# Four fused transformer sub-layers on one core: the last delta chunk taken one sequence at a time and without its state, the output weights split inside the attention, and first tokens normalised by halves of the sequences

## The reference

```python
x = x + delta_attention(layernorm(x))   # 6 heads of 64, causal conv, gated delta rule, Wo
x = x + nvfp4_ffn(layernorm(x))         # 4-bit weights, gelu(gate) * up, hidden 4096
x = x + latent_attention(layernorm(x))  # 16 heads, latent 64, rotary, softmax over 1024, wo
x = x + sparse_ffn(layernorm(x))        # silu(gate) * up, two largest of each four kept, hidden 2048
```

```python
S = S * exp(g_t)
u = b_t * (v_t - k_t @ S)
S = S + outer(k_t, u)
o_t = (q_t * scale) @ S
o = o * rsqrt(mean(o*o) + EPS) * o_norm_w * silu(gate)      # then @ Wo.T
```

## Time and profile before

| | |
|---|---|
| median of 3 runs | 3021.94 us (3019.69 to 3023.62) |
| profiled execution | 3021.52 us, span 3019.7 us |
| mean granted clock of TensorE | 0.961 of full speed |
| PE busy | 2829.2 us, 94% of the span |
| DVE, ACT, POOL busy | 56%, 36%, 26% |
| DMA | 114.92 MB, mean 38 GB/s |

### The profile page before, as it was taken

The page is one execution under the profiler, slowest core; times in us unless marked ns, Lnnn a source line. Parts: engine busy times, 40 slices in busy tenths (PEclk is TensorE's granted clock), DMA queues, the critical chain, the costliest instruction groups (busy, mean ns, idle before and its releaser), DMA issues. The chain is left out here.

```text
span 3019.7 us, 37185 instructions
## 1 busy us (share of the span) xinstructions
PE 2829.2 (94%) x13750; PEld 2332.9 (77%) x13750; DVE 1702.2 (56%) x2585; ACT 1073.9 (36%) x1615; POOL 791.4 (26%) x832
## 2 busy tenths in 40 slices
PE   7966988799999999999999689999999899999998
PEld 7846777678888888888888558888888677888887
DVE  6864677564445444454543666666666256545554
ACT  3343343131121211111211357777777522212221
POOL 0038686100000000000000157777778510000000
PEclk9967999899999999999999889999999999999999
DMA  2243232110000100000100121111110100101001
GB/s 85 104 115 70 52 73 49 46 42 21 22 21 21 42 21 21 21 21 21 35 7 1 40 64 43 43 43 36 43 36 22 43 14 28 42 1 42 14 14 42
DMA packets 96418, 114.92 MB, mean 38 GB/s; under 512 B 47072, under 2 KB 73696, under 8 KB 94624
## 3 DMA queue, kind: packets, MB, share of 16 engines
q1 hardware_dynamic: 96288, 113.20, 12.7%
HBM read 86.16 MB, written 26.74 MB: 37 GB/s over the span
## 5 line engine op out<-in xcount | busy, mean ns | idle before, releaser
L2017 POOL TENSOR_TENSOR att_p_lo<-att_probs,att_p_hi 128x768 fp32r<-128x768 f32 x256 | 467.3, 1837 | 147.3 <-ACT att_p_hi L2074 146.1
L2170 DVE TENSOR_REDUCE att_top<-att_q_scores 128x1 f32<-128x1024 f32 x250 | 305.5, 1222 | 220.0 <-PE att_q_scores L2277 187.9
L271 DVE TENSOR_TENSOR fp_hidden<-fp_gelu,fp_up 128x512 f32<-128x512 f32 x128 | 88.0, 687 | 440.2 <-PE fp_up L75 377.2
L2085 ACT ACTIVATE att_probs<-att_k_scores 128x1024 f32<-128x1024 f32 x256 | 262.9, 1027 | 160.9 <-PE att_k_scores L2295 159.5
L1751 POOL MEMSET lat_power<- 128x16 f32 x1 | 0.1, 111 | 1051.8 <-POOLq L52 1051.8
L256 DVE TENSOR_TENSOR k_stream<-k_stream,fp_down 128x512 f32<-128x512 f32 x256 | 175.4, 686 | 89.6 <-PE fp_down L75 86.1
L335 ACT ACTIVATE fp_gelu<-fp_gate 128x512 f32<-128x512 f32 x128 | 76.4, 597 | 420.3 <-PE fp_gate L75 419.4
L2074 ACT CAST att_p_hi<-att_probs 128x768 fp32r<-128x768 f32 x256 | 211.7, 827 | 0.0
L73 PE MATMUL fp_gate<-fp_feat_hi,fp_w_hi 128*128 128x512 f32 x512 | 200.6, 392 | 4.0 <-DVE fp_feat_lo L241 4.0
L2277 PE MATMUL att_q_scores<-att_k_stack,att_q_stack 128*128 128x512 f32 x500 | 187.1, 456 | 14.5 <-DMA att_q_stack<-att_k_stack 10.6
L75 PE MATMUL fp_gate<-fp_feat_hi,fp_w_lo 128*128 128x512 f32 x512 | 200.2, 391 | 0.0
(11 more groups left out here) (350 smaller groups left out, 6537.3 us busy)
## 6 DMA issues: line engine op xcount, KB each, us to landing
f_early<-codes SPq DMA_DIRECT2D x16, 768.0 KB
f_early<-scales SPq DMA_DIRECT2D x16, 768.0 KB
la_values<-w_sparse SPq DMA_DIRECT2D x10, 1024.0 KB, 5.2
f_early<-qkv SPq DMA_DIRECT2D x16, 576.0 KB, 6.2
att_q_stack<-rotated SPq DMA_DIRECT2D x128, 64.0 KB, 2.6
att_k_stack<-rotated SPq DMA_DIRECT2D x128, 64.0 KB, 2.6
qkv<-f_early SPq DMA_DIRECT2D x12, 512.0 KB, 2.9
k_stream<-hidden SPq DMA_DIRECT2D x4, 1024.0 KB, 10.3
```

The lines of the kernel that those rows point to most:

```text
L2017: pool.tensor_tensor(p_lo[:, buffer, :], probs[:, slot, 0:SPLIT], p_hi[:, buffer, :].bitcast(F32), ALU.subtract).then_inc(lo_done, 1)
L2085: act.activation(probs[:, t, :], k_scores[:], ACT.Exp).then_inc(exp_done, 1)
L2170: dve.tensor_reduce(top[buffer][:, STACK + t:STACK + t + 1], scores[:], AX.XY, ALU.max, negate=True).then_inc(max_done, 1)
```

## The change

It has four parts.

1. Last delta chunk: `decay_state`, `add_to_state` and `add_state` are left out for chunk 7 (no later chunk reads the state). Its sums, gate, logarithms and normalisation are done for sequence 0 and then for sequence 1. The second `first_codes` stands after `corrected_values` as before. The turned outputs go to other PSUM banks (3 and 4), so that PE waits for one sequence's `gated` only. SP issues the codes and scales before the residual of chunk 6.
2. First tokens of both feed-forwards: the token blocks are taken in the order 0, 2, 1, 3, and `EARLY` is now the first half of both sequences (tiles 0 to 3 and 8 to 11). The first four tiles of the 4-bit stage are scaled before that stage (`scale_first`), into the storage of the delta rule's blocks; the Gelu table is loaded there too.
3. `w_out` is loaded into the rotary tables' storage during the attention's pass 6, and split in its last pass: for each of the four heads a 128x512 cast on ACT at t = 3 and a 128x512 subtraction on DVE at t = 4. Silu's table is loaded at the start of `project_out`.
4. Sparse stage: in the first group `scale` of block tb + 2 stands after the four products of block tb. Several buffers share storage with buffers of the attention.

```diff
@@ delta_rule, sync @@
+                if c == LAST:
+                    sp.wait_ge(qk_ps, FOURS * CHUNKS)
+                    load_codes(sp, fp4, codes, scales, 0)
                 if c:
                     load_residual(c - 1)
...
-            sp.wait_ge(qk_ps, FOURS * CHUNKS)
-            load_codes(sp, fp4, codes, scales, 0)
             load_residual(CHUNKS - 1)
@@ delta_rule, tensor @@
-                    else:
-                        pe.wait_ge(gated, 2 * c + 2)
-                        pe.wait_ge(state_done, 6 * CHUNKS)
...
-                add_to_state(c, ahead)
+                if c != LAST:
+                    add_to_state(c, ahead)
@@ delta_rule, scalar @@
-            output_logs(CHUNKS - 1)
-            split_output(CHUNKS - 1)
+            act.wait_ge(o_small, 4 * LAST)
+            for b in range(BATCH):
+                last_square(b)
+                last_logs(b)
+            split_output(LAST)
+            act.preload_act_table(ACT.Gelu_apprx_tanh)
@@ delta_rule, vector @@
+            def scale_first():
+                dve.wait_ge(token_norm.rstd_done, 1)
...
+                for j, i in enumerate(tiles_of(0)):
+                    dve.tensor_scalar(fp4.normed[:, j, :], stream[:, i, :], token_norm.mean[:, i:i + 1],
+                                      token_norm.rstd[:, i:i + 1], ALU.subtract, ALU.mult).then_inc(fp4.normed_done, 1)
...
                 corrected_values(c)
-                if c == CHUNKS - 1:
-                    first_codes(1, (0, 1))
-                gate_output(c)
-                decay_state(c)
-                add_state(c)
-            output_sums(CHUNKS - 1)
-            normalise_output(CHUNKS - 1)
+                if c != LAST:
+                    gate_output(c)
+                    decay_state(c)
+                    add_state(c)
+            first_codes(1, (0, 1))
+            last_sums(0)
+            last_gate(0)
+            last_normalise(0)
+            last_sums(1)
+            last_gate(1)
+            last_normalise(1)
             first_codes(1, (2,))
-            low_output(CHUNKS - 1)
-            token_stats(CHUNKS - 2)
+            low_output(LAST)
+            token_stats(LAST - 1)
+            scale_first()
@@ nvfp4_feed_forward, scalar @@
-            act.preload_act_table(ACT.Gelu_apprx_tanh)
@@ softmax_heads, sync, scalar, vector @@
+                if g == QUAD * (PASSES - 2) + 1:
+                    sp.wait_ge(piece_step, 3 * ROTATED)
+                    sp.dma_start(o32.rearrange("p (k n) -> p k n", k=KT), w_out.rearrange("(k p) n -> p k n", p=P))\
+                      .then_inc(o_in, 16)
...
+                        if t == 3 and last:
+                            high_weights(j)
...
+                        if t == 4 and last:
+                            low_weights(j)
                         if t == TURN and not (last and j == QUAD - 1):
                             copy_top(g + 1, False)
@@ project_out, scalar, vector, tensor @@
-            act.wait_ge(o_in, 16)
-            act.copy(o_hi[:], o32[:]).then_inc(o_hi_done, 1)
+            act.preload_act_table(ACT.Silu)
...
-            pe.wait_ge(o_lo_done, 1)
@@ sparse_feed_forward, vector @@
-                    for i in next_tiles:
-                        scale(i)
...
+                    if first and tb + 2 < BLOCKS:
+                        if tb == 0:
+                            dve.wait_ge(norm.rstd_done, 2)
+                        scale(tb + 2)
```

More of the change, by code:

```diff
@@ L348, in _ @@
             high_weights(0, 0, 1)
[L349 to L350 removed]
+            high(0)
             body(0, True, False)
@@ L2697, in body @@
                     act.wait_ge(kept, 4 * n + 4)
-                    act.copy(h_hi[:], hidden[:]).then_inc(h_hi_done, 1)
-            for i in range(SUB):
-                high(i)
+                    act.copy(h_hi, hidden).then_inc(h_hi_done, 1)
+            high(0)
             body(0, True, False)
```

284 lines of the change are left out of this document (167 added, 117 removed).

## The result

| | before | changed |
|---|---|---|
| median | 3021.94 us (11 executions, 3014.32 to 3028.03) | 3009.42 us (11 executions, 3001.32 to 3012.33) |
| profiled execution, span | 3021.52 us, 3019.7 us | 3001.32 us, 2999.5 us |
| mean granted clock | 0.961 | 0.964 |
| PE busy | 2829.2 us, 94% | 2825.2 us, 94% |

The changed kernel is faster: ratio 0.9958, 95% interval 0.9949 to 0.9968, which is 12.5 us of the 21.95 that I had forecast. 3009.4 lies outside the range of 2995 to 3007.

The account below looks back on a forecast made before the run. PE, busy 94% of the span, was taken as the bound. From 3021.52 us, less 6.5, 3.4, 1.3, 8.45 and 4.6, plus 2.3, gives 2999.6; with the median 0.4 above, 3000.0 us, range 2995 to 3007 (8 in 10).

Parts of the forecast that it names:

- what is paid for it lies in the last pass: Last attention pass: casts and subtractions of `w_out` quarters cost 2.3 us, bounds 0.5 and 4.4.
- if the last pass grows by over 4 us: Last attention pass: growth above this size was one of three signs that the prediction is wrong.
- codes: Last delta chunk: earlier issue lets scales land sooner, PE idles less and outputs keep their clock; 6.5 us saved.
- chain: Behind the last delta outputs: first projection matmul follows after 6.75 us, not 10.13; 3.4 us saved.
- table load: Head of the stage after the delta rule: load moves from ahead of the weight cast to ACT's idle time; 1.3 us saved.
- The boundary of `project_out`: Start of `project_out`: PE no longer waits for load, cast and subtraction of `w_out`; 8.45 us saved.
- The sparse scaling: Sparse stage: tiles scaled earlier, so PE goes on at about 2502.1, not 2506.73; 4.6 us saved, bounds 3.5 and 5.4.
- A new wait at a boundary: Rival, 12%: a stage's head is bounded by something the old wait covered; up to 6 us together, near 3005.
- The transfer was not late: Rival, 12%: delta chunk 7's scales still land at 570 or later; 6.5 us gone, 3006.5.
- Half clock over `project_out`: Rival "Slower", 2%: `project_out` begins in small pieces and TensorE stays at half clock; some 43 us, result 3043.

Follow-up runs that it names:

- storage_swap: Changed kernel with the sparse stage's third high weight part and `h_hi` exchanging places in SBUF; 3007.8 us, one execution.
- no_part3: Changed kernel with `w_out` loaded, cast and subtracted at the start of `project_out`, ahead of PE's transposes; median 3008.5 us, ratio 0.9964.
- sub_behind_copy: Changed kernel with the last pass's quarter subtraction of the output weights behind `copy_top` instead of ahead of it; median 3001.6 us, ratio 0.9939.
- half_ahead: Changed kernel with each last-pass quarter subtraction cut into 256-column halves, one ahead of `copy_top`, one behind; median 3011.3 us, ratio 0.9964.
- split_incs_first: Changed kernel with `w_out` split whole at `project_out`'s start, DVE's opening increments ahead of its wait for the cast; median 3004.0 us, ratio 0.9944.

## Why the prediction came out wrong

**The step that failed** is the one headed "what is paid for it lies in the last pass": "A 128x512 quarter [...] is 0.5 on ACT and 0.6 on DVE", so 2.3 us back, with 4.4 as the upper bound. ACT's part measured 0.62. DVE's 0.6 was scaled from an operation that ran while POOL was idle (2.29 us for four quarters); in the pass POOL is at work, and the quarter takes 1.9. In place of 2.3 the runs show 7.4 us (the mean of C over the nine profiles with a whole quarter ahead of the copy, 94.8, against 87.4). Of that 3.2 us are two waits of PE for `copy_top` (I had priced a delay in three heads), 1.7 are time lost at half clock behind the first wait, in all nine profiles, and 3.4 more are lost behind the second wait in four of the nine; I had not priced the clock there. Some 0.9 us are shorter waits of PE in the last two heads. The bound was too narrow because both its ends used the same row. I had named this in the text as the thing that would prove me wrong ("if the last pass grows by over 4 us").

**Not in the sum at all**: column F, 1.8 us, the down products of the sparse stage; and G, 1.1 us, where the last down products run at half clock for 5 to 6 us in most profiles instead of 3.5, after the same wait of 4.3. Part of the change is the new place of buffers, which I had costed at nothing without saying so. What slows the down products is not settled. That G is due to the change is only likely: both before are at 20.6, twelve of the fourteen others at 21.5 or more, but storage_swap and no_part3 at 20.7.

**Right in mechanism and size**: codes, chain and table load, 11.2 us together: B falls from 110.4 (two profiles) to 98.3 (nine), 12.2. Within it the outputs fell by 2.9 us by the clock between the first two profiles (3.1 forecast), the chain to 6.4 us (6.75), the table 1.14 (1.3). Less sure is the codes' own share: with only their order undone the tail grows by 3.6 and 5.0 us, and I had put 6.5. The boundary of `project_out`: 8.45 forecast, 8.7 measured. The sparse scaling: 4.6 forecast; E, which also holds `project_out`, fell by 3.8, undoing the part costs 3.0 to 3.8, and the blocks themselves show 5.5 less the 1.0 given back.

**Right sum, without a split**: I gave the chain's 3.4 us as one sum for state and sequences. Undone alone, the state costs 4.1 us and the sequences 0.57, so nearly all of it is the state's.

**The sum as measured**, differences of the means: A plus 1.6, B minus 12.2, C plus 7.4, D minus 8.7, E minus 3.8, F plus 1.8, G plus 1.1: minus 12.8, and the medians differ by 12.5. Of the 9.1 us that this is off the forecast, 5.1 are C, 2.9 are F and G, 1.6 are A (which I take for chance, with only two profiles of before), 0.8 are E, and B and D were 1.3 better than forecast. (Means are over the profiles in which the stage is as in the changed kernel; G and A over all fourteen.)

**The rivals.** "A new wait at a boundary" had the splits in the last pass among its prices, with 2.1 us; that is the nearest. The transfer was not late (0 to 1.2 us of waiting for the scales in all profiles with the new order, against 4.97 and 5.94 before). Half clock over `project_out` lasted 6 us.

**A version that beats both**: sub_behind_copy, 3001.6 us, one line moved. It is close to what I had forecast for the change, since its pass pays 0.6 us against the mean of before.

## What to carry to other kernels

Before moving a VectorE operation with two SBUF operands, or a copy between SBUF buffers, look at what GpSimd does at that moment: add what is left of GpSimd's running operation to the price, and never put such an operation ahead of one for which PE waits. A duration measured at a quiet boundary is not its price in a busy loop. And a wait of PE can cost more than its length: price it with a stretch of half clock behind it. Here that stretch came behind the first wait in all nine profiles and behind the second in four of them, so that one profile can't tell its size.

## What the runs showed of the hardware

- A 128x512 subtraction of SBUF operands on VectorE would take 0.57 us with GpSimd idle (an estimate: a quarter of the 2.29 us of four quarters), and took 0.98, 1.48 or 1.9 us when it started 1.38, 0.89 or 0.47 us into a GpSimd subtraction of 1.84 us (sub_behind_copy and the changed kernel); with 256 columns it took 1.64 (half_ahead). A copy of 128x256 in SBUF took 0.28 us or, started 0.56 us into a GpSimd subtraction, 1.49. In the other order GpSimd's two copies took 2.62 us instead of 1.17 (split_incs_first).
- A wait of PE of 1.6 us between busy stretches was followed by clock 0.56 over 3.4 us in one profile and 0.60 over 4 us in another (1.7 us lost in each of nine profiles); the second such wait, 22 us later, by nothing in five of the nine and by 3.4 us lost in four, in one of them 0.84 over 16 us.
- Down products with the same shapes and full clock took 390 ns in one layout of buffers and 391 to 395 in another; exchanging two of the buffers did not change it.
- Two executions of the changed kernel reached one point some 500 us in 10.1 us apart, with a mean granted clock of 0.90 and 0.89 up to there; the fourteen profiles, alike in code up to that point, differ by 13.6 us. The time lost below full clock (one less the granted clock, times the length) makes up 6.4 of the 10.1 us and 12.2 of the 13.6.
